# Scan steps that alternate between channel pairs, one spread of C for two steps, and B's rows brought to all partitions by DMA

## What is computed

```python
deltaA = jnp.exp(jnp.einsum('bld,dn->bldn', delta, A))
deltaBu = jnp.einsum('bld,bln,bld->bldn', delta, B, u)
...
h = h * dA_t + dBu_t
y = jnp.einsum('bdn,bn->bd', h, C_t)
...
y = y + u * D
out = (y * silu(res)) @ W_out + x
```

## Time and profile before

| | |
|---|---|
| three runs | 984.05, 985.33 and 987.88 us, median 985.33 |
| profiled execution | 984.03 us, of this 982.2 us in the span of the profile |
| TensorE matmul | 870.8 us busy (89%), 4643 instructions |
| TensorE weight load | 652.0 us (66%) |
| VectorE | 643.3 us (65%) |
| ScalarE | 383.9 us (39%) |
| GpSimd | 358.9 us (37%) |
| DMA | 67.69 MB in 22196 packets, mean 69 GB/s |

### The profile page before, as it was taken

One profiled execution on the slowest core, in us unless ns is written; L12 is line 12 of the kernel. 1 busy time (PEld: TensorE's weight loads), 2 busy tenths in 40 slices (PEclk: granted clock), 3 DMA queues, 4 the chain that ended last, 5 costly groups with the idle time before them and its releaser, 6 DMA issues.

```text
span 982.2 us, 13012 instructions
## 1 busy us (share of the span) xinstructions
PE 870.8 (89%) x4643; PEld 652.0 (66%) x4668; DVE 643.3 (65%) x1378; ACT 383.9 (39%) x828; POOL 358.9 (37%) x393
## 2 busy tenths in 40 slices
PE   6897675988999998889999998888999998789997
PEld 5675344754787786744787886653788786426886
DVE  6332799795355998895355999875355999764333
ACT  4111743326236443426326443417226544243111
POOL 5202485120042875220043875220042876000322
PEclk9897877999999999999999999979999999879999
DMA  6204000002023330301024330302022330300452
GB/s 217 110 0 175 0 1 0 1 14 98 1 81 113 126 113 2 107 29 82 1 81 145 97 111 1 108 1 110 1 68 69 94 109 17 108 1 1 129 153 84
DMA packets 22196, 67.69 MB, mean 69 GB/s; under 512 B 2860, under 2 KB 4780, under 8 KB 21492
## 3 DMA queue, kind: packets, MB, share of 16 engines
q1 hardware_dynamic: 21876, 66.80, 20.8%
q10 hardware_dynamic: 256, 0.07, 0.0%
HBM read 65.74 MB, written 1.05 MB: 68 GB/s over the span
## 4 chain that ended last, share of the span: by engine, by line
PE 49%; DVE 19%; POOL 12%; issue 12%; ACT 7%; DMA 1%; ACTq 1%; POOLq 0%; DVEq 0%; SPq 0%
PE B L779 22%; PE F L779 21%; POOL arena L465 7%; DVE arena L1430 5%; DVE nmx L1501 3%; PE B L1068 3%; POOL spare L550 2%; ACT big L746 2%; POOL arena L475 2%; PE F L808 1%; DVE arena L1270 1%; DVE arena L1442 1%; PE F L790 1%; POOL rs L447 1%; PE B L1149 1%
## 5 line engine op out<-in xcount | busy, mean ns | idle before, releaser
L779 PE MATMUL B<-spare,mw 128*128 128x256 f32 x880 | 209.3, 382 | 0.0
L779 PEld LDWEIGHTS B<-spare,mw 128*128 128x128 f32 x880 | 166.5, 191 | 24.8 <-issue 2.6
L550 POOL TENSOR_TENSOR spare<-q_t 128x256 f32<-128x256 f32 x112 | 82.0, 738 | 193.3 <-DVE q_t L1567 134.2
L1430 DVE TENSOR_TENSOR_SCAN arena<-F,arena 128x512 f32<-128x512 f32 x128 | 149.5, 1207 | 3.7 <-ACT F L702 2.3
L465 POOL TENSOR_TENSOR arena<-du,arena 128x1024 f32<-128x1024 f32 x60 | 140.9, 2360 | 9.8 <-PE F L779 8.5
L702 ACT ACTIVATE F<-delta,a_neg 128x255 f32<-128x255 f32 x256 | 109.9, 467 | 72.6 <-DVE arena L1430 72.6
L779 PE MATMUL B<-mw,spare 128*128 128x256 f32 x448 | 115.4, 381 | 1.2 <-POOL spare L550 1.2
L779 PE MATMUL F<-arena,ident 128*128 128x256 f32 x400 | 105.1, 406 | 1.4 <-POOL arena L475 1.0
L768 ACT ACTIVATE q_t<-B 128x256 f32<-128x256 f32 x112 | 42.0, 381 | 159.2 <-PE B L779 152.6
L1562 DVE SCALAR_TENSOR_TENSOR q_t<-q_t,B 128x256 f32<-128x256 f32 x112 | 46.6, 416 | 77.7 <-ACT q_t L768 77.4
L779 PEld LDWEIGHTS B<-mw,spare 128*128 128x128 f32 x448 | 84.2, 190 | 15.9 <-POOL spare L550 3.9
(11 more groups left out here) (228 smaller groups left out, 1284.0 us busy)
## 6 DMA issues: line engine op xcount, KB each, us to landing
mw<-in_w_moe SPq DMA_DIRECT2D x112, 384.0 KB, 3.1
room<-in_w_f SPq DMA_DIRECT2D x4, 2544.0 KB, 9.1
room<-in_w_l SPq DMA_DIRECT2D x4, 768.0 KB, 7.1
w_m<-in_w_m SPq DMA_DIRECT2D x1, 2112.0 KB
room<-in_w_l SPq DMA_DIRECT2D x4, 512.0 KB, 4.9
x_t<-in_x_t SPq DMA_DIRECT2D x4, 256.0 KB, 3.3
x_tok<-in_x_tok SPq DMA_DIRECT2D x4, 256.0 KB, 6.4
y<-x SPq DMA_DIRECT2D x4, 256.0 KB, 2.2
```

Of the source, the lines that this page charges most:

```text
L550: g.tensor_tensor(hid1[0:r, m % HID_RING, :], hraw[0:r, m % 3, :], crs[0:r, int(m >= MTE), :], ALU.mult)\
L779: return t_.matmul(dst, lhsT, rhs, start=start, stop=stop, skip_group_check=True)
L1430: v.tensor_tensor_scan(h, F[i][:, :], h, 0.0, ALU.mult, ALU.add)\
```

## The change

Steps alternate: step n is now pair n % 2 with k = n // 2, so two steps in a row use the same rows of B and of C. One spread of C serves both, 8 per entry. The two pairs' sums are now both open through the scan: pair 0 keeps F[3], pair 1 takes K[2]. So the expert blocks of all but the last entry have two banks for gate and up instead of three, and pair 1's first sum waits until the attention of the back half is done with K[2]. Both gated outputs stand in `u1`.

B's rows no longer go over TensorE and ScalarE. In `d1`, when `bct` is copied, SP issues 16 transfers, each of which reads one row of 256 floats from one partition and writes it to all 128 partitions of `b_rep`; each k has a semaphore. `bct` moves to a place that no state overwrites. The phase in which SP issues a load of expert weights is three blocks later, with the same wait.

All four orders are written anew. On TensorE be9 and be10 now stand before `d1`, none stand between `d1` and `s0`, be11 to be13 follow `s0` and be15 to be19 follow `s4`. The maxima start one phase earlier.

```diff
-AFTER = {"load": 2, "qkv": 4, "at2": 2, "at3": 2, "at5": 1, "at6": 3, "at7": 2, "oa": 2, "ob": 7, "xa": 1, "xb": 1,
-         "xc": 3, "xd": 4, "fa1": 1, "fa2": 1, "fa3": 2, "fg2": 1, "fg4": 1, "fg5": 1, "fd1": 3, "fd2": 3, "m1": 2,
-         "m2": 1, "m5": 1, "d2": 2, "d4": 2, "s2": 3, "s3": 1, "s4": 2, "s6": 2, "s7": 2, "s8": 2, "s10": 1, "s11": 2,
-         "s13": 1}
...
-AFTER_PE = {"load": 2, "qkv": 1, "at2": 2, "at3": 1, "at4": 2, "at5": 2, "at6": 1, "at7": 7, "oa": 2, "ob": 5, "xa":
-            1, "xb": 1, "xc": 1, "xd": 6, "fa1": 1, "fa2": 1, "fa3": 1, "fg0": 1, "fg1": 1, "fg4": 1, "fg5": 1, "fd1":
-            3, "fd2": 1, "fd3": 2, "m1": 1, "m2": 2, "m3": 1, "d1": 1, "d2": 1, "d3": 1, "d4": 1, "s0": 1, "s1": 1,
-            "s2": 1, "s3": 1, "s4": 1, "s5": 2, "s6": 1, "s7": 2, "s9": 3, "s10": 1, "s11": 1, "s13": 1}
...
+AFTER = {"load": 2, "qkv": 4, "at1": 3, "at4": 1, "at5": 2, "at7": 4, "ob": 9, "xa": 1, "xb": 2, "xc": 2, "xd": 4,
+         "fa1": 1, "fa2": 2, "fa3": 1, "fg2": 2, "fg3": 1, "fg4": 2, "fd1": 2, "fd3": 1, "m1": 3, "m4": 2, "m5": 2,
+         "s0": 1, "s1": 2, "s3": 2, "s4": 3, "s6": 3, "s7": 1, "s8": 1, "s9": 1, "s10": 2, "s11": 1, "s15": 1}
...
+AFTER_PE = {"load": 2, "qkv": 1, "at1": 1, "at2": 2, "at3": 1, "at4": 2, "at5": 1, "at6": 2, "at7": 3, "oa": 2, "ob":
+            8, "xa": 1, "xb": 1, "xc": 1, "xd": 6, "fa1": 1, "fa2": 1, "fa3": 2, "fg0": 1, "fg2": 1, "fg3": 3, "fg5":
+            1, "fd1": 1, "fd2": 1, "m1": 3, "m2": 1, "m3": 1, "m4": 1, "m5": 1, "s0": 3, "s3": 1, "s4": 5, "s6": 1,
+            "s7": 1, "s8": 3, "s10": 1, "s11": 2, "s13": 1}
...
-        dtr, bct, bcr = arena[:, 9216:9472], arena[0:32, 9472:9728], arena[0:32, 9728:9984]
+        dtr, bct, bcr = arena[:, 9216:9472], arena[0:32, 10240:10496], arena[0:32, 9728:9984]
...
+        rep_in = [sem(f"rep_in{k}") for k in range(NK)]
...
+        def gate_bank(b, m):
+
+            return K[m % (3 if b == B - 1 else 2)]
+
+        def y_bank(dp):
+
+            return K[2] if dp else F[3]
...
+                if ph == "d1":
+                    sp.wait_ge(*af.at("bct", b))
+                    for j in range(NS):
+                        k, half = divmod(j, 2)
+                        sp.dma_start(b_rep[:, k, half * S:half * S + S], bct[j:j + 1, :].unsqueeze(1).to_broadcast([1, P, S]))\
+                            .then_inc(rep_in[k], 16)
...
-                if ph in BE and BE.index(ph) + MW_RING < MT1:
-                    m = BE.index(ph)
+                if ph in BE and 3 <= BE.index(ph) < MT1 - MW_RING + 3:
+                    m = BE.index(ph) - 3
                     sp.wait_ge(*pb.at(f"down{m}", b))
                     sp.dma_start(mw[:, m % MW_RING, :], ins["w_moe"][m + MW_RING])\
...
-                dp, k = divmod(n, NK)
+                k, dp = divmod(n, 2)
                 if dp == 0:
-                    pool.wait_ge(*af.at(f"rep{k}", b))
+                    pool.wait_ge(rep_in[k], b * 32 + 32)
...
+                if n == 4:
+                    pool.wait_ge(*pf.at("dl1", b))
...
-                if ph == "d3":
-                    replicate(b, 0)
...
                     scan_decay(b, 0)
-                    for k in (1, 2, 3):
-                        replicate(b, k)
                 if ph in STEPS[:-1]:
                     scan_decay(b, STEPS.index(ph) + 1)
-                    if ph in STEPS[:2]:
-                        n = STEPS.index(ph)
-                        for k in (4 + 2 * n, 5 + 2 * n):
-                            replicate(b, k)
...
-                dp, k = divmod(n, NK)
+                k, dp = divmod(n, 2)
...
-            def replicate(b, k):
-
-                if k == 0:
+            def spread_c(b, n):
+
+                if n == 0:
                     pe.wait_ge(*df.at("bcp", b))
                     pe.wait_ge(*af.at("bct", b))
-                if k == 1:
-                    pe.wait_ge(*af.at("delta0", b))
-                if k >= 2:
-                    pe.wait_ge(*af.at(f"rep{k - 2 if k < 4 else k - 1}", b))
-                spread(F[rep_bank(k)], 2 * k, f"rep{k}")
-
-            def spread_c(b, n):
-
-                if n == 0:
-                    pe.wait_ge(*af.at("rep2", b))
                 else:
                     pe.wait_ge(*df.at(f"hc{n - 1}", b))
-                spread(F[2], NS + 2 * (n % NK), f"c{n}")
...
-                dp, k = divmod(n, NK)
+                k, dp = divmod(n, 2)
                 if n == 0:
-                    pe.wait_ge(*af.at(f"rep{NK - 1}", b))
-                if n == NK:
-                    pe.wait_ge(*df.at("y_read0", b))
+                    pe.wait_ge(*af.at("delta0", b))
+                if n == 1 and later(b):
+                    pe.wait_ge(*db.at("x4_read", b - 1))
...
-                        last = mm(F[3][:, i * S:i * S + S], ident[:, :], state(n)[:, i, s * S:s * S + S],
+                        last = mm(y_bank(dp)[:, i * S:i * S + S], ident[:, :], state(n)[:, i, s * S:s * S + S],
...
-                if ph == "d3":
-                    for k in range(3):
-                        replicate(b, k)
-                if ph == "d4":
-                    replicate(b, 3)
                 if ph in STEPS:
                     n = STEPS.index(ph)
-                    spread_c(b, n)
-                    if n < 2:
-                        for k in (4 + 2 * n, 5 + 2 * n):
-                            replicate(b, k)
+                    if n % 2 == 0:
+                        spread_c(b, n)
                     if n >= 2:
                         sum_states(b, n - 2)
+                    if n == NSTEP - 1:
+                        sum_states(b, NSTEP - 2)
                 if ph == "u1":
-                    sum_states(b, NSTEP - 2)
                     sum_states(b, NSTEP - 1)
                     scan_out(b, 0)
...
+                    r = 3 if b == B - 1 else 2
+                    if m >= r:
+                        pe.wait_ge(*db.at(f"gu{m - r}", b))
...
-                    if n == NK + 1:
-                        gated_output(b, 0)
-                    dve.wait_ge(*pf.at(f"c{n}", b))
+                    dve.wait_ge(*pf.at(f"c{n - n % 2}", b))
...
+                    gated_output(b, 0)
                     gated_output(b, 1)
...
-                dve.wait_ge(*pf.at(f"y{NK * i + NK - 1}", b))
+                dve.wait_ge(*pf.at(f"y{NSTEP - 2 + i}", b))
```

More of the change, by code:

```diff
@@ L66 @@
              BACK[BACK.index("ba1"):])
-AFTER = {"load": 2, "qkv": 4, "at2": 2, "at3": 2, "at5": 1, "at6": 3, "at7": 2, "oa": 2, "ob": 7, "xa": 1, "xb": 1,
-         "xc": 3, "xd": 4, "fa1": 1, "fa2": 1, "fa3": 2, "fg2": 1, "fg4": 1, "fg5": 1, "fd1": 3, "fd2": 3, "m1": 2,
-         "m2": 1, "m5": 1, "d2": 2, "d4": 2, "s2": 3, "s3": 1, "s4": 2, "s6": 2, "s7": 2, "s8": 2, "s10": 1, "s11": 2,
-         "s13": 1}
-AFTER_POOL = {"load": 7, "qkv": 1, "at0": 3, "at1": 12, "at4": 10, "oa": 1, "fa1": 3, "fa3": 2, "fg1": 4, "fd2": 1,
-              "m1": 4, "m3": 3, "d2": 1, "s0": 2, "s2": 3, "s3": 1, "s4": 2, "s5": 1, "s6": 1, "s7": 2, "s8": 1, "s9":
-              1, "s10": 1, "s12": 1, "s13": 2, "u1": 1}
-AFTER_PE = {"load": 2, "qkv": 1, "at2": 2, "at3": 1, "at4": 2, "at5": 2, "at6": 1, "at7": 7, "oa": 2, "ob": 5, "xa":
[3 rows of a table removed]
-AFTER_DVE = {"load": 2, "at0": 1, "at2": 1, "at3": 2, "at4": 1, "at5": 3, "at6": 1, "at7": 7, "oa": 2, "xa": 1, "xb":
[3 rows of a table removed]
+AFTER = {"load": 2, "qkv": 4, "at1": 3, "at4": 1, "at5": 2, "at7": 4, "ob": 9, "xa": 1, "xb": 2, "xc": 2, "xd": 4,
+         "fa1": 1, "fa2": 2, "fa3": 1, "fg2": 2, "fg3": 1, "fg4": 2, "fd1": 2, "fd3": 1, "m1": 3, "m4": 2, "m5": 2,
+         "s0": 1, "s1": 2, "s3": 2, "s4": 3, "s6": 3, "s7": 1, "s8": 1, "s9": 1, "s10": 2, "s11": 1, "s15": 1}
+AFTER_POOL = {"load": 2, "qkv": 2, "at0": 1, "at3": 3, "at4": 1, "at5": 2, "at6": 3, "oa": 1, "ob": 3, "xa": 3, "xc":
+              3, "fa2": 6, "fg0": 1, "fg4": 3, "fg5": 1, "fd1": 8, "fd2": 4, "fd3": 1, "m5": 2, "d3": 3, "s3": 4,
+              "s5": 3, "s6": 1, "s7": 2, "s8": 1, "s9": 1, "s10": 2, "s11": 2, "s12": 1, "s15": 1}
+AFTER_PE = {"load": 2, "qkv": 1, "at1": 1, "at2": 2, "at3": 1, "at4": 2, "at5": 1, "at6": 2, "at7": 3, "oa": 2, "ob":
[3 rows of a table added]
+AFTER_DVE = {"load": 2, "at0": 1, "at1": 1, "at2": 2, "at3": 1, "at4": 2, "at5": 1, "at6": 1, "at7": 4, "oa": 6, "xa":
[3 rows of a table added]
 IDLE_FIRST = {"xa": 7, "fa1": 19}
@@ L346, in state @@
             return hb[:, r, :, :]
-        def rep_bank(k):
-            return 2 if k in (0, 2) else 3
         def max_bank(b, n, i):
@@ L703, in scan_decay @@
                     ins_.then_inc(af.step(f"dA{n}_{i}"), 1)
-            def replicate(b, k):
-                act.wait_ge(*pf.at(f"rep{k}", b))
-                copy(b_rep[:, k, :], F[rep_bank(k)][:, :], af, f"rep{k}")
             def back(b, ph):
@@ L767, in back @@
                     r = P if m < MT1 - 1 else HALF
-                    a.activation(thg[0:r, m % 3, :], K[m % 3][0:r, 0:S], ACT.Tanh, scale=0.5)\
```

(30 more changed lines are left out.)

## The result

The changed kernel took 1157.67 us (median of 4 runs, 1155.96 to 1159.72) where the kernel before, measured beside it, took 985.0: 1.1785 times as long, 95% interval 1.1733 to 1.1836. The forecast of 973.8 and its range were wrong. Rival A came true, but not at its own price of 1060. The sentence on the Trainium skill beside it had some 1,170.

A forecast was written before the change was run, and what follows sets the result against it. VectorE was taken to bound the scan, TensorE the 85.2 us stretch of each period. Gains of 2.8 us in batch 0 and 8.7 in three later periods came off 984.0; with 1.3 to the median, 973.8, range 951 to 1,000.

The forecast's parts named there:

- Rival A: B's transfers: reading one partition is slow, 45 GB/s, and be14's weights queue behind; 1060 us, chance 0.18.
- The sentence on the Trainium skill: B's transfers: four partitions on one port gave 27.6 GB/s, so 4.7 us each, 76 in all, and some 1,170.
- I take the store, the nearest in packet size: B's transfers priced like y's store: 285 GB/s, 0.46 us each, 7.4 us for all 2 MB.
- The row with few partitions on one side: The other bound for B's transfers: a 4 KB transfer of maxima at 45 GB/s, kept as a rival.
- The issue on SP: SP's queue: sixteen transfers of B's rows issued at 0.43 us each, 6.9 us.
- Batch 0, 2.8 us: Gain in the first batch: 0.6 us for B copies plus 2.2 for moving pair 0's gated output.
- the 0.6 for the copies: Batch 0: 0.6 us gained by dropping ScalarE's copy of B ahead of the first decay.
- The start of the scan: Two more blocks before d1 delay the copy about 5.2 us, but the first scan starts where it did: zero, within 1 us.
- 1.0 for steps 0 and 1: Scan start in each later period: 1.0 us gained without the B spreads and copies that delay these steps.
- 1.4 for the gated output: Each later period: moving pair 0's gated output from step 9 to the scan's end gains 1.4 us net.
- Two banks, 0.5: Gate and up, five blocks after step 4's spread: up to 1.6 us a period lost, 0.5 taken.
- Orders elsewhere, 1.0: Attention stage, maxima one pair earlier, in a window with 7.1 us of idle TensorE: 1.0 us gained in each of three periods.

The follow-up runs named there:

- e3: The changed kernel with its 16 transfers reading a constant tile from 128 partitions instead of B's rows from one partition each: 976.4 us (one run).
- e4: The changed kernel with the 16 transfers issued in row order 0, 4, 8, 12, 1, 5, ...: 1070.88 us (one run).
- e6: The changed kernel with B's 16 rows stored to device memory and read back by eight transfers of 256 KB: 976.64 us, ratio 0.9953.
- e10: The kernel before with only B's rows through device memory and expert weight loads issued three blocks later: 987.94 us, ratio 1.0028.
- e8: The changed kernel with B's rows through device memory and the scan's expert blocks spread evenly, one or two a step: 979.53 us, ratio 0.9964.
- e2: The changed kernel with B over TensorE and ScalarE, and the orders and weight-load place of the kernel before: 993.28 us, ratio 1.0088.

## Why the prediction was wrong, point by point

- **The step that failed** is "I take the store, the nearest in packet size". One-partition reads went at 27.5 GB/s, not 285; 4.77 us each, not 0.46. e3 shows that the side read makes all of it. The row with few partitions on one side, at 45 GB/s, was the nearer one in kind, and I set it aside because it was small. e4 says in kind why: rows 0 to 3 don't overlap, rows of different groups of four do. By the Trainium skill (SBUF — State Buffer, "Door 1: The DMA port swizzle") four partitions on one port give 27.6 GB/s; the trace agrees, at 27.5 for one partition.
- **Rival A's mechanism was right in each place:** the first input late, be14 starved. Its price of 1060 was not. It set be14's weights at about 50 us after the copy for 2.9 us a transfer; at 4.77 it is 71.6, measured. Its point of decision, 16 us for 2 MB, agrees with what ran: e3 (10 us) hid the transfers, e4 (34 us) did not. Its chance of 0.18 was too low: the two bounds lay a factor of six apart, on either side of the point of decision.
- **The issue on SP** was counted at 0.43 us each. Where the data is quick it is 0.60 (e3). In the changed kernel the first two take 0.49 and 0.60 us, the third 2.13, and from the fourth on SP is held at the pace of the data, 4.77.
- **Batch 0, 2.8 us:** right without the slow read: 3.0 in e6, 3.9 in e3, up to the next batch's start. Of the 0.6 for the copies, e10 shows 0.2.
- **The start of the scan, "zero, to within 1":** right in one period of three. In e6 the first scan comes 6.0 instead of 10.6 us after the copy, and the copy comes 5.0 us later in the second period (122.19 instead of 117.17 us; 5.2 forecast) but 6.0 later in the first and third, at a mean clock of 0.97. So the scan starts 0.4 us later in one period and 1.4 in the other two.
- **1.0 for steps 0 and 1, 1.4 for the gated output:** right in place. VectorE's two waits for C of 0.57 and 0.54 us are gone, there is no step of 6.84 us, and the last gated output starts without a wait at 608.65, as late after the last scan as one product takes.
- **Two banks, 0.5:** mis-sized. e6 waits 0.81, 0.99 and 0.69 us in the steps where the bursts stand, 2.5 us a period. I had bounded only the C of step 6. Thus the scan got shorter by 0.2 us, not 1.9. It is the bursts more than the banks: e8, with the same two banks and the blocks spread out, has a scan of 69.3 us, almost 2 us shorter. And "in the stages before the scan that is covered" holds with the new orders alone: with before's it is 2.2 us (e2).
- **Orders elsewhere, 1.0:** 0.2 in one period (5.0 against 5.2), and 0.8 lost in each of the other two (6.0 against 5.2).
- Had the read been fast, the forecast of 973.8 would have looked right: e6 and e3 took 976.6 and 976.4, inside its range of 962 to 980. That is luck. The 2.8 us of batch 0 came, but the 8.7 of the three later periods did not: the two full periods of e6 are 1.2 and 0.3 us longer than those of the kernel before, and of the 5.3 us won after them 4.8 are what the kernel before lost to its clock in the profile on which the forecast was built.

## What to carry to other kernels

To price a transfer, count the partitions that each side reaches, and take the row that is nearest in that, not in packet size: here the same 128 KB to the same 128 partitions took 4.77 us from one partition and 0.60 from 128. What lies between was not measured. If a row of a tile must go to all partitions, a store of 16 KB and a read back from device memory is ten times quicker to issue here than reading one partition 128 times. Ask too what stands behind a transfer in its queue: of 181 us, 67 went when loads of weights that had nothing to do with B were let through. And when the two ends of an unknown price lie on either side of the point from which it decides, the range has to hold both.

## What the runs showed that I had not expected

SP is held back in issuing from the third slow transfer on (0.49, 0.60, 2.13, then 4.77 us each), so slow transfers block the whole queue almost at once. Reads that take turns among four groups of four partitions overlap only 1.8 times. And a stage of the same instructions takes 117.17 or 122.00 us by whether TensorE's clock falls to half within it, in the kernel before too: differences of 5 us between single profiles say little until the granted clock of each stage has been compared.
